# Means of the first two tiles from a chunk sum of xT, and a later place for the first P products

## The reference

```
xn  = (x - mean(x)) / sqrt(var(x) + 1e-5)
q   = xn @ Wq.T + bq            # of 32 heads of 128 only every 4th is used
s   = elu(q) + 1                # 8 heads x 128
a   = (s @ M) / (s . z + 1e-6)  # each head repeated 4 times
out = x + repeat(a) @ Wo.T + xn @ (w * w_scale) + b
```

## Time and profile before

| | us |
|---|---|
| median of 3 runs (lowest, highest) | 243.72 (243.65, 243.77) |
| the profiled execution | 243.56 |
| its span, first to last instruction | 241.7 |
| PE busy in the span | 234.1 (97%) |
| DVE, ACT, POOL busy | 178.0, 119.6, 108.4 |

### The profile page before, as it was taken

One profiled execution on the slowest core, in us unless ns is written; L12 is line 12 of the kernel. 1 busy time (PEld: TensorE's weight loads), 2 busy tenths in 40 slices (PEclk: granted clock), 3 DMA queues, 4 the chain that ended last, 5 costly groups with the idle time before them and its releaser, 6 DMA issues.

```text
span 241.7 us, 3385 instructions
## 1 busy us (share of the span) xinstructions
PE 234.1 (97%) x1030; PEld 186.7 (77%) x1030; DVE 178.0 (74%) x266; ACT 119.6 (49%) x276; POOL 108.4 (45%) x108
## 2 busy tenths in 40 slices
PE   8699999998999999999999999999999999999995
PEld 2488788885776788888888888888888888788885
DVE  2889695897998669887687694958666778995631
ACT  2654626628648923655463526455463747341110
POOL 1058734756271815553434326263403629657500
PEclk9999999999999999999999999999999999999999
DMA  7999999999370211424252515221212223244441
GB/s 225 405 417 411 383 242 225 216 217 217 94 252 5 53 51 52 127 54 126 53 168 53 161 50 169 52 91 42 88 52 73 56 75 108 76 136 136 133 174 44
DMA packets 21985, 34.83 MB, mean 144 GB/s; under 512 B 5200, under 2 KB 13136, under 8 KB 20816
## 3 DMA queue, kind: packets, MB, share of 16 engines
q1 hardware_dynamic: 19344, 26.63, 33.4%
q0 software_dynamic: 1376, 6.82, 13.4%
q10 hardware_dynamic: 1248, 1.18, 1.8%
HBM read 22.02 MB, written 4.19 MB: 108 GB/s over the span
## 4 chain that ended last, share of the span: by engine, by line
PE 33%; issue 31%; POOL 18%; DVE 8%; SPq 4%; DMA 2%; ACT 2%; ACTq 1%; POOLq 0%; DVEq 0%
POOL e_and_sz L313 9%; POOL xT L288 5%; PE attn_ps L793 4%; PE attn_ps L794 4%; PE attn_ps L795 4%; SPq L219 4%; POOL x L321 3%; PE q_ps L793 3%; PE q_ps L795 3%; PE q_ps L794 3%; DVE aT_lo L654 2%; PE dense_ps L793 2%; PE dense_ps L795 2%; PE dense_ps L794 2%; DMA xT<-in_xT 2%
## 5 line engine op out<-in xcount | busy, mean ns | idle before, releaser
L313 POOL TENSOR_TENSOR e_and_sz<-s,z_b 128x512 f32<-128x512 f32 x32 | 42.0, 1340 | 40.3 <-DVE den L633 40.2
L441 ACT ACTIVATE s<-s,rden 128x128 f32<-128x128 f32 x128 | 39.2, 389 | 40.5 <-DVE rden L637 40.5
L793 PE MATMUL attn_ps<-P_hi,aT_hi 128*128 128x512 f32 (+1 forms) x128 | 49.8, 389 | 0.5 <-DVE aT_lo L654 0.5
L795 PE MATMUL attn_ps<-P_hi,aT_lo 128*128 128x512 f32 (+1 forms) x128 | 49.1, 383 | 0.0
L794 PE MATMUL attn_ps<-P_lo,aT_hi 128*128 128x512 f32 (+1 forms) x128 | 49.0, 383 | 0.0
L793 PE MATMUL q_ps<-WqT_hi,xT_hi 128*128 128x512 f32 x104 | 42.1, 405 | 0.3 <-DVE s L628 0.3
L795 PE MATMUL q_ps<-WqT_hi,xT_lo 128*128 128x512 f32 x104 | 40.6, 390 | 0.0
L794 PE MATMUL q_ps<-WqT_lo,xT_hi 128*128 128x512 f32 x104 | 40.5, 389 | 0.0
L288 POOL TENSOR_TENSOR xT<-xT,mean_b 128x512 f32<-128x512 f32 x13 | 18.3, 1408 | 37.8 <-ACT mean_b L390 31.2
L621 DVE SCALAR_TENSOR_TENSOR q_ps<-q_ps,rstd,bq_b 128x512 f32<-128x512 f32 x28 | 21.0, 753 | 19.3 <-PE q_ps L795 19.3
L793 PEld LDWEIGHTS attn_ps<-P_hi,aT_hi 128*128 128x128 f32 x128 | 24.1, 188 | 6.2 <-issue 0.9
(11 more groups left out here) (82 smaller groups left out, 365.3 us busy)
## 6 DMA issues: line engine op xcount, KB each, us to landing
x<-in_WoT POOLq DMA_DIRECT2D x6, 1024.0 KB, 10.6
x<-in_x SPq DMA_DIRECT2D x16, 256.0 KB, 3.9
xT<-in_xT SPq DMA_DIRECT2D x16, 256.0 KB, 4.1
aT<-s SPq DMA_DIRECT2D x124, 32.0 KB, 1.9
out<-x SPq DMA_DIRECT2D x15, 256.0 KB, 2.3
MT<-s SPq DMA_DIRECT2D x96, 32.0 KB, 1.9
x<-in_WoT SPq DMA_DIRECT2D x2, 1024.0 KB, 14.0
s<-in_WqT SPq DMA_DIRECT2D x2, 512.0 KB, 7.1
```

The costliest lines, as they stand in the source:

```text
L313: nc.gpsimd.tensor_tensor(sz_eps[:, :, h * D // 2:(h + 1) * D // 2].rearrange("p g (j c) -> p j g c", j=2), by_quarter(sbuf_s[:, t % SRING ...
L441: last = nc.scalar.activation(a_g, a_g, ACT.Copy, scale=rden[:, t % 2, g:g + 1])
L793: nc.tensor.matmul(out, x_hi, w_hi, start=start, stop=False)
L795: return nc.tensor.matmul(out, x_lo, w_hi, start=False, stop=stop)
```

## The change

**Means of tiles 0 and 1.** DVE sums the four chunks of xT[t] (`sum_chunks`), and PE multiplies the sum by a matrix that holds 1/512 everywhere (`mean_of_columns`), which gives each row's mean on all partitions. POOL fills that matrix first. The mean of tile 1 goes to the bank of q 2, the others to that of the means. The statistics of tiles 0 and 1, still needed for rstd, come after those of tile 2.

**Loads.** xT[0] comes first and x[0], x[1] come after all of Wq and tile 2; Wq is loaded in halves of a chunk; ACT issues one half of Wq and xT[1]. Later, x[4] and xT[4] come ahead of the second half of Wo, x[5] to xT[6] ahead of M and b.

**Order.** The first 48 products are reordered, the warm-up products are 6 and 3 with the mean between them. POOL scales its half of w before the first three rstd. P0 to P4 and their copies and splits come later. In the tail ACT copies tile 11 before it issues the transfers for tile 12, and DVE takes the last denominator after the split of tile 11.

```diff
+        def mean_in(t):
+            return (q_ps[2] if t == 1 else mean_ps)[:, 0:P]
+        def moments_before(t):
+            return [1, 2, 0][t] if t <= 2 else t
...
-            load_x(0)
             load_xT(0)
+            load_wq_half(0, 1)
             load_wq_half(1, 0)
-            load_x(1)
             load_wq_half(1, 1)
-            load_xT(1)
-            load_wq(2)
+            load_wq_half(2, 0)
+            load_wq_half(2, 1)
+            load_wq_half(3, 0)
+            load_wq_half(3, 1)
             load_x(2)
             load_xT(2)
-            load_wq(3)
+            load_x(0)
+            load_x(1)
...
             load_wo(0)
-            load_wo(1)
-            sp.dma_start(MT[:], MT_d).then_inc(M_in, 16)
             load_x(4)
             load_xT(4)
+            load_wo(1)
+            load_x(5)
+            load_xT(5)
             sp.dma_start(z_b[:], z_d.unsqueeze(0).to_broadcast([P, E])).then_inc(z_in, 16)
+            load_x(6)
+            load_xT(6)
+            sp.dma_start(MT[:], MT_d).then_inc(M_in, 16)
             sp.dma_start(b_b[:], b_d.unsqueeze(0).to_broadcast([P, HID])).then_inc(b_in, 16)
-            for t in range(5, FIRST_LENT):
+            for t in range(7, FIRST_LENT):
...
+            nc.gpsimd.memset(mean_weights[:], 1.0 / HID).then_inc(mean_weights_set, 1)
...
+            scale_w()
             rstd_of(0)
             rstd_of(1)
             rstd_of(2)
-            scale_w()
...
+            def sum_chunks(t):
+                dve.wait_ge(xT_in[t], 16)
+                nc.vector.reduce_sum(x_sum[:, t, :], xT[:, t, :, :].rearrange("p k r -> p r k"), AX.X).then_inc(x_sum_ready, 1)
...
+            def mean_of_columns(t):
+                if t == 0:
+                    pe.wait_ge(mean_weights_set, 1)
+                pe.wait_ge(x_sum_ready, t + 1)
+                nc.tensor.matmul(mean_in(t), mean_weights[:], x_sum[:, t, :], start=True, stop=True
+                                 ).then_inc(mean_filled, 1)
...
             product_q(5, 1)
-            product_P(0)
-            product_q(6, 0)
-            product_P(1)
             spread_mean(7)
             product_dense(5)
+            product_q(6, 0)
+            product_P(0)
+            product_P(1)
+            product_q(6, 1)
             product_P(2)
-            product_q(6, 1)
             product_P(3)
```

More of the change, by code:

```diff
@@ L103, in retrieval_and_dense @@
         xT_in = [sem(f"xT_in{t}") for t in range(T)]
-        wq_half_in = [sem(f"wq_half_in{i}") for i in range(4)]
-        wq_in = [sem(f"wq_in{k}") for k in range(2, K)]
+        wq_half_in = [sem(f"wq_half_in{i}") for i in range(2 * K)]
         wo_in = [sem(f"wo_in{j}") for j in range(J)]
@@ L464, in _ @@
             nc.scalar.activation(table_loaded[:], warm[:, 0:1], ACT.Copy)
-            for h in range(2):
-                act.dma_start(WqT_raw[:, 0, halves(h)], WqT_d[0, 0][:, halves(h)]).then_inc(wq_half_in[h], 16)
+            act.dma_start(WqT_raw[:, 0, halves(0)], WqT_d[0, 0][:, halves(0)]).then_inc(wq_half_in[0], 16)
+            act.dma_start(xT[:, 1, :, :].rearrange("p k r -> p (k r)"), xT_d[1]).then_inc(xT_in[1], 16)
+            copy_wq_hi(0, 0)
             copy_first_xT_hi(0)
-            copy_wq_hi(0, 0)
+            copy_first_xT_hi(1)
             copy_wq_hi(0, 1)
             copy_wq_hi(1, 0)
-            copy_first_xT_hi(1)
             copy_wq_hi(1, 1)
+            copy_wq_hi(2, 0)
             copy_xT_hi(1)
-            copy_wq_hi(2, 0)
             copy_wq_hi(2, 1)
@@ L478, in _ @@
             cast_w(0)
+            cast_w(1)
             copy_xT_hi(2)
-            cast_w(1)
             copy_wd_hi(0)
@@ L683, in _ @@
             split_wq_lo(3, 0)
+            split_wq_lo(3, 1)
+            moments(0)
             center(2)
-            split_wq_lo(3, 1)
             split_xT_lo(2)
+            moments(1)
             scale_w()
@@ L705, in _ @@
             make_s(1, 1)
+            add_dense(1)
             split_xT_lo(4)
-            add_dense(1)
             make_s(2, 0)
@@ L729, in _ @@
             make_s(5, 0)
+            turn_blocks(1)
+            make_s(5, 1)
+            denominator(2)
+            add_dense(5)
+            add_bias(6, 0)
             split_P_lo(0)
-            make_s(5, 1)
-            add_bias(6, 0)
             split_P_lo(1)
-            turn_blocks(1)
-            add_dense(5)
-            denominator(2)
+            make_s(6, 0)
+            split_xT_lo(7)
+            add_bias(6, 1)
+            moments(8)
             split_P_lo(2)
-            make_s(6, 0)
-            add_bias(6, 1)
-            split_xT_lo(7)
+            denominator(3)
+            make_s(6, 1)
             split_P_lo(3)
-            moments(8)
-            denominator(3)
             add_dense(6)
-            make_s(6, 1)
-            split_P_lo(4)
             split_aT_lo(0)
             turn_blocks(2)
+            split_P_lo(4)
             for t in range(LEAD, T):
@@ L877, in _ @@
             pe.wait_ge(warm_set, 1)
-            keep_busy(8)
-            pe.wait_ge(consts_set, 3)
-            spread_mean(0)
             keep_busy(6)
+            mean_of_columns(0)
+            keep_busy(3)
             hi_hi(0, 0, 0)
+            hi_hi(0, 1, 0)
+            lo_hi(0, 0, 0)
+            lo_hi(0, 1, 0)
+            mean_of_columns(1)
             hi_lo(0, 0, 0)
[L884 to L888, removed]
-            hi_lo(0, 1, 0)
[L890 to L893, removed]
-            hi_lo(1, 0, 0)
-            hi_lo(0, 0, 1)
-            hi_hi(1, 1, 0)
-            hi_lo(1, 1, 0)
-            hi_lo(0, 1, 1)
+            for h in range(2):
+                hi_hi(0, h, 1)
+                lo_hi(0, h, 1)
+            hi_lo(0, 1, 0)
             hi_hi(0, 0, 2)
             lo_hi(0, 0, 2)
-            lo_hi(1, 0, 0)
-            lo_hi(1, 1, 0)
+            hi_lo(0, 0, 1)
+            for h in range(2):
+                hi_hi(1, h, 0)
+                hi_lo(1, h, 0)
+            hi_lo(0, 1, 1)
             for h in range(2):
@@ L905, in _ @@
                 hi_lo(1, h, 1)
-                lo_hi(1, h, 1)
-            hi_lo(0, 0, 2)
             hi_hi(0, 1, 2)
             lo_hi(0, 1, 2)
-            hi_lo(0, 1, 2)
-            spread_mean(2)
+            for h in range(2):
+                lo_hi(1, h, 0)
+                lo_hi(1, h, 1)
             for h in range(2):
@@ L914, in _ @@
                 lo_hi(1, h, 2)
-                hi_lo(1, h, 2)
+            pe.wait_ge(consts_set, 3)
+            spread_mean(2)
             for t in range(2):
                 for h in range(2):
-                    hi_hi(t, h, 3)
-                    lo_hi(t, h, 3)
-                    hi_lo(t, h, 3).then_inc(q_filled, 1)
+                    hi_lo(t, h, 2)
+            for h in range(2):
+                hi_hi(0, h, 3)
+                lo_hi(0, h, 3)
+                hi_lo(0, h, 3).then_inc(q_filled, 1)
+            for h in range(2):
+                hi_hi(1, h, 3)
+                lo_hi(1, h, 3)
+                hi_lo(1, h, 3).then_inc(q_filled, 1)
             product_q(2, 0)
```

93 lines of the change are left out of this document (43 added, 50 removed).

## The result

The changed kernel takes 249.06 us (median of 4 runs, 248.34 to 250.75) against 243.69 for the kernel before: a ratio of 1.0229, 95% interval 1.0188 to 1.0271. Forecast were 245.5 us and a range up to 247.8. The direction was right and the place was right; the size was not: 5.4 us are lost, not 1.8.

The account below looks back on a forecast made before the run. PE was taken to bound the kernel, by its start and missing operands. The profiled 243.56 plus 2.05 at dense(5) minus 0.3 in the tail gave 245.31, with 0.16 added 245.5 us; range 243.7 to 247.8.

Parts of the forecast that it names:

- the step that decides: PE's dense(5), moved ahead of P0, waits for add_dense(4) on DVE until 59.96: a loss of 2.05 us.
- B: Rival, no change: the chain of Wo adds moves with its earlier start, add_dense(4) 1.5 us earlier; 244.0 us, chance 0.10.
- the estimate of 4.4: Time in us for one 1 MB Wo add by the Trainium skill's rule: 2.0 us plus bytes at 436 GB/s.
- the split 1.1 us earlier: Term in the forecast's bounds 244.4 to 246.8: split_xT_lo(6) on DVE, ahead of add_dense(4), coming earlier.
- P0 to P4 at 0: Copies and splits after these products follow closer on ACT and DVE; PE has about 1 us to spare at each.
- the tail at -0.3: Tile 11's 0.52 us PE wait goes (-0.5); the later denominator gives some back: between -0.5 and +0.3 us.
- The start: PE's first product at 5.4 instead of 6.80, with a 0.7 us sum; tile 1's 0.96 us wait goes.
- The lead: PE about 1.7 us ahead after 48 products, 0.3 at the first dense product, then worth nothing before dense(5).
- The wait of about 1 us for the split of tile 2: PE waits at tile 2 because DVE's split may have to let POOL's weight scaling end, at 19.0.
- C: Rival, clearly slower: x(7) lands late behind MT and b, delaying DVE's statistics; 247.5 to 249.5 us, chance 0.14.

## Why the prediction was wrong, step by step

From the changed kernel's 249.06 a ladder of medians leads down. Each step is the price of an edit with all that the edit brings, not of one cause alone: filling the wait 1.9, add_dense(4) early in place of the fill 1.3 (247.16 to 245.83; the wait goes, and waits at P products come), the tail 0.95 (to 244.88), the other order of P products, dense(5) and q(6) 2.4 (to 242.45). Against the kernel before, the last stands 1.1 to the good.

- **Right: the step that decides.** PE waits before dense(5) for add_dense(4), over 3 us; no wait stays before P0; split_xT_lo(6) is late and long as forecast (56.25 and 2.31 us, against 55.71 and 2.34). The price of the wait alone, worked out as 2.05 us, is 60.54 + 4.56 - 62.47 = 2.63 in the trace, because the addition came 0.52 later than it stood. That the adds would not come earlier with an earlier start was right too (the last is issued at 53.36 against 52.81), and with it B falls. Beside the other transfers an add took 10.5 us from issue to landing in the median and 9.8 at the least, not the estimate of 4.4. (The forecast's own range counts the split 1.1 us earlier where the bound given for it is 1.65; nothing came to hang on that.)
- **Wrong: the wait was priced at its length.** "PE idles 59.96 - 56.90 = 3.1 us" went into the sum as the delay of dense(5), 2.05 us, and no more. The step lacked the clock: after the idling PE runs at half of it. That is 2.5 us in the trace, about 1.9 in the median. The text had the two levels before it, at the start's warm-up products, and did not ask what a wait of 3 us does to the clock in mid-kernel.
- **Wrong: P0 to P4 at 0, "with 0.5 as the bound of loss".** It is 1.3 us in the trace around P6 and P7, and 2.0 at P2 to P7 where PE is not held up before. For the slack of 1 us per product the prediction names no row. P2 and P3 can lose it because the new order puts P0 and P1 back to back. P6 lost it because the change also puts split_P_lo(4) behind the two splits of tile 0 and a turning, 80.46 to 85.06 on DVE, of which the first split took 1.82 us (see the last section); put back ahead of them, it leaves P7 to wait.
- **Wrong: the tail at -0.3.** It is +0.8 in the trace. The removed 0.52 us was credited to ACT's copy alone. The later denominator was named, but followed only to tile 15's turning; it costs 1.4 us through make_a(15) on ACT and the copy of tile 12 behind it.
- **The start.** The sum over chunks takes 1.02 us, not 0.7, and the first product comes at 6.14, not 5.4; tile 1's 0.96 us did go. The lead was 1.18 us at tile 2's first product (19.03 against 20.21), not 1.7, then 0.86 at the first dense product (24.94 against 25.80), not 0.3, and 0.60 at 55; it was worth nothing, as said. The wait of about 1 us for the split of tile 2 did not come: PE loses 0.24 us there.

```profile
3.24 1.02 DVE L573 TENSOR_REDUCE x_sum<-xT 128x128 f32<-128x512 f32 x1 [2.31 <-DMA xT<-in_xT]
```

- **C** (x(7) late) did not happen: DVE takes its statistics at 49.68, waiting for no DMA.

With the wait and the clock right, but the P's and the tail as predicted, the sum would have been 243.72 + 2.6 + 1.9 - 0.3 = 247.9; the P's and the tail make up the rest to 249.06.

## What to carry to other kernels

A wait that is put in front of a busy PE can cost more than its length, as all three waits of 2.40 us and more before dense(5) did here: price the passes behind it at the lower clock, or let PE do something in it. When a product is moved ahead, list what its buffer waits for on the engine that frees it, and look whether that instruction itself could stand earlier: here moving one line on DVE took back 3.2 of the 5.4 us lost. And a lead counts only where no operand arrives at a time of its own, which the lead does not move: such waits have to go before an earlier start can gain anything.

## What was not expected of the hardware

The clock fell for a wait of 2.40 us too (P0 to P4 alone moved), and not equally in every run; behind the 1.82 us before P0 (P0 to P4 as before) the profiled run shows 1.00. In the first of these, the kernel's runs lie 3.1 us apart, and their mean clocks between 0.986 and 1.000.

Where DVE and POOL start within hundredths of a microsecond of each other, which of the two is held up can set a microsecond. In the changed kernel DVE's two splits for tile 0 and POOL's centring of tile 8 begin 0.02 us apart, and the splits take 3.52 us in all. DVE:

```profile
80.46 3.52 DVE L663 TENSOR_TENSOR aT_lo<-aT,aT_hi 128x512 fp32r<-128x512 f32 x2
```

POOL beside it:

```profile
80.44 1.29 POOL L300 TENSOR_TENSOR xT<-xT,mean_b 128x512 f32<-128x512 f32 x1 [4.25 <-ACT mean_b L403]
```

With the wait filled they again begin 0.02 us apart, POOL first by its row as before, and the splits take 2.37, the centring 1.84 instead of 1.29. DVE:

```profile
77.86 2.37 DVE L663 TENSOR_TENSOR aT_lo<-aT,aT_hi 128x512 fp32r<-128x512 f32 x2
```

POOL beside it:

```profile
77.84 1.84 POOL L300 TENSOR_TENSOR xT<-xT,mean_b 128x512 f32<-128x512 f32 x1 [4.25 <-ACT mean_b L403]
```

The difference lies in the first of the two splits: 1.82 us in the changed kernel, 0.68 with the wait filled. In the changed kernel the split is held up, with the wait filled the centring. The first case gives P6 and P7 their 0.83 us of waits, the second none. The rule of the Trainium skill (SBUF — State Buffer, Who interferes with whom) says that whoever issues first holds the shared port. The trace of the changed kernel agrees with it; in the other, POOL's row begins 0.02 us ahead and POOL is held up all the same, so the starts that the traces show do not tell who got the port, and what decides it is not shown.
